# A down product of tokens by channels, added to x1 straight from its PSUM banks

## The reference, cut to what matters

```python
sel = sigmoid(einsum('bsd,ed->bse', x1, expert_sel))
scores = relu(einsum('bsd,edh->bseh', x1, keys))            # the up product, 16 experts of 128
out = einsum('bseh,ehv,bse->bsv', scores, values, sel)      # the down product, summed over experts
x = _layernorm(x1 + out, axis=-1)
```

## Time and profile before

| | |
|---|---|
| median of the runs | 1125.85 us (1124.51 to 1129.42) |
| the profiled execution's span | 1119.6 us |
| PE, matmuls | busy 93%, 5228 of them |
| DVE, ACT, POOL | busy 71%, 47%, 21% |
| mean granted clock of PE | 0.969 of full |
| `down_bank` matmuls | 1536, some 0.40 us each, overlapping |
| copies into `oT` | 597 ns median, two a group |

### The profile page before, as it was taken

How to read it: one execution, slowest core, us unless ns; L and a number is a source line. 1 busy time by engine, 2 the same in 40 slices (tenths; PEclk the granted TensorE clock), 3 DMA queues, 4 the chain that set the end, 5 groups by cost and what they waited for, 6 DMA issues and landing times.

```text
span 1119.6 us, 17488 instructions
## 1 busy us (share of the span) xinstructions
PE 1039.2 (93%) x5228; PEld 871.5 (78%) x5228; DVE 793.8 (71%) x1811; ACT 525.6 (47%) x1223; POOL 234.0 (21%) x280
## 2 busy tenths in 40 slices
PE   5775689999998999989999899999999899999996
PEld 4564568888887888878888788878888788888885
DVE  6844368687875788758787577857887687877564
ACT  5632265346533565235653356334653356534342
POOL 2321222222212111111212121221112221222221
PEclk9987889999999999989999899999999999999999
DMA  5021000020001100011000110011000110000000
GB/s 182 23 95 57 0 2 20 2 76 20 2 21 39 56 1 10 9 40 56 1 19 3 55 38 1 19 39 56 0 1 19 40 56 1 19 1 20 2 20 20
DMA packets 12089, 32.01 MB, mean 29 GB/s; under 512 B 1792, under 2 KB 2048, under 8 KB 12032
## 3 DMA queue, kind: packets, MB, share of 16 engines
q1 hardware_dynamic: 12032, 31.42, 8.3%
HBM read 22.50 MB, written 8.39 MB: 28 GB/s over the span
## 4 chain that ended last, share of the span: by engine, by line
PE 85%; issue 7%; DVE 4%; ACT 2%; POOL 1%; DMA 0%; DVEq 0%; ACTq 0%; SPq 0%; POOLq 0%
PE down_bank L996 30%; PE up_bank L996 30%; PE ring_bank L996 9%; PE qk_bank L996 7%; PE g_bank L996 4%; PE ring_bank L1114 1%; PE ring_bank L1095 1%; DVE gated L970 1%; PE ring_bank L1079 1%; PE ring_bank L1105 1%; PE ring_bank L1104 1%; ACT gated_h L522 1%; PE ring_bank L1060 0%; ACT oT L522 0%; DVE gated_l L980 0%
## 5 line engine op out<-in xcount | busy, mean ns | idle before, releaser
L522 ACT ACTIVATE gated_h<-gated 128x512 fp32r<-128x512 f32 x256 | 161.3, 630 | 443.8 <-DVE gated L970 443.8
L503 POOL PARTITION_BROADCAST sel_all<-sel_rows x240 | 192.2, 803 | 745.1 <-DVE gated L970 718.9
L970 DVE SCALAR_TENSOR_TENSOR gated<-up_bank,sel_all 128x512 f32<-128x512 f32 x256 | 176.1, 688 | 135.8 <-PE up_bank L996 83.2
L996 PE MATMUL down_bank<-gated_h,vals_h 128*128 128x512 f32 x512 | 213.0, 416 | 25.0 <-ACT oT L522 18.7
L980 DVE TENSOR_TENSOR gated_l<-gated,gated_h 128x512 fp32r<-128x512 f32 x256 | 178.9, 699 | 47.0 <-ACT gated_h L522 47.0
L996 PE MATMUL up_bank<-x1T_h,keys_h 128*128 128x512 f32 x512 | 204.4, 399 | 0.0
L996 PE MATMUL down_bank<-gated_h,vals_l 128*128 128x512 f32 x512 | 204.2, 399 | 0.0
L996 PE MATMUL down_bank<-gated_l,vals_h 128*128 128x512 f32 x512 | 204.1, 399 | 0.0
L996 PE MATMUL up_bank<-x1T_h,keys_l 128*128 128x512 f32 x512 | 203.5, 398 | 0.0
L996 PE MATMUL up_bank<-x1T_l,keys_h 128*128 128x512 f32 x512 | 202.3, 395 | 0.0
L996 PEld LDWEIGHTS down_bank<-gated_h,vals_h 128*128 128x128 f32 x512 | 98.2, 192 | 46.2 <-ACT oT L522 19.9
(11 more groups left out here) (159 smaller groups left out, 1720.0 us busy)
## 6 DMA issues: line engine op xcount, KB each, us to landing
xT_raw<-in_xT SPq DMA_DIRECT2D x16, 512.0 KB, 3.8
x_raw<-in_x SPq DMA_DIRECT2D x16, 512.0 KB, 4.5
out<-z SPq DMA_DIRECT2D x32, 256.0 KB, 2.5
oT<-in_keys SPq DMA_DIRECT2D x4, 512.0 KB, 4.0
z<-in_values SPq DMA_DIRECT2D x4, 512.0 KB, 5.4
sel_rows<-sel SPq DMA_DIRECT2D x64, 8.0 KB
x<-in_wqk SPq DMA_DIRECT2D x1, 512.0 KB, 3.4
sel_all<-in_b_qk SPq DMA_DIRECT2D x1, 256.0 KB, 5.2
```

Of the source, the lines that this page charges most:

```text
L503: nc.gpsimd.partition_broadcast(sel_all[:, e % 2], row, P).then_inc(sel_spread, 1)
L522: return nc.scalar.activation(dst, src, ACT.Copy, **kw)
L970: V.scalar_tensor_tensor(out=gated[:], in0=up_bank[s % 2][:], scalar=0.0, in1=sel_all[:, s % 2], op0=ALU.max, op1=ALU.mult).then_inc(gate_ ...
L996: last = mm(dst, lhs, rhs, start=start and i == 0, stop=stop and i == n - 1, **kw)
```

## The change

The down product is turned round. gated is now stationary, 128 tokens at a time (t, 0 to 3), and the 256 channels of vals are streamed, so that the sums stand as tokens by channels: bank a of `down_bank` holds the token blocks 2a and 2a + 1 side by side. A step has 12 matmuls of 256 columns in place of 6 of 512. The first matmul of each bank clears it; the second block's region is then free to be written.

Since the sums stand as the output does, nothing is copied or transposed. DVE adds x1 to each bank straight into `z` (`add_zs`, stage ZA) in the first step behind the group: step 17 for the first group of a batch, step 1 of the next iteration for the second. Its wait is `down_made`, and PE waits for `z_added` before it writes the bank anew. The rest of OT stays where it was, as stage ZN, and takes no ring bank. ACT's copies and PE's transposes go. In the last iteration both adds come first, the first of them as soon as half of the last product is made. `w_room`, of the same size, takes the place of `oT` as landing place.

```diff
 LOOP = dict(
     plan={
-        0: [("QT", 2)], 1: [("QT", 3)], 2: [("OT", 0), ("Y", 4)], 3: [("OT", 1)], 4: [("Y", 5)],
+        0: [("QT", 2)], 1: [("ZA", 0), ("ZA", 1), ("QT", 3)], 2: [("ZN", 0), ("Y", 4)], 3: [("ZN", 1)], 4: [("Y", 5)],
...
-        16: [("GG", 5)], 17: [("QK", 7)], 18: [("GG", 6)], 19: [("KS", 0), ("OT", 0), ("GG", 7)],
-        20: [("OT", 1)], 21: [("KV", 0), ("QT", 0)], 22: [("QT", 1)], 23: [("Y", 0)],
+        16: [("GG", 5)], 17: [("ZA", 0), ("ZA", 1), ("QK", 7)], 18: [("GG", 6)], 19: [("KS", 0), ("ZN", 0), ("GG", 7)],
+        20: [("ZN", 1)], 21: [("KV", 0), ("QT", 0)], 22: [("QT", 1)], 23: [("Y", 0)],
...
-LAST = dict(plan={1: [("OT", 0), ("OT", 1)]}, split_xT={}, split_x={}, bias_x={}, scale_q={},
+LAST = dict(plan={1: [("ZA", 0), ("ZA", 1), ("ZN", 0), ("ZN", 1)]}, split_xT={}, split_x={}, bias_x={}, scale_q={},
...
-RING_KINDS = ("QT", "Y", "XT", "LG", "OT", "KS", "KV")
+RING_KINDS = ("QT", "Y", "XT", "LG", "KS", "KV")
...
         @block.scalar
-                if (s - LAG) % E == E - 1 and step_exists(it, s, LAG):
...
-                        act.wait_ge(down_made, f + 1)
-
-                    at_least(act, o_transposed, 2 * grp)
...
-                    for m in range(M if not last_iteration(it) else 1):
-                        copy(oT[:, m], down_bank[m][:]).then_inc(o_copied, 1)
...
         @block.vector
+            def add_zs(it, s):
+                for kind, a, off in planned(it, s, ("ZA",)):
+                    n = out_pair(it, off, a)
+                    t = GT * (off % G) + 2 * a
+                    if last_iteration(it) and a == 0:
+                        dve.wait_ge(last_half_made, 1)
+                    else:
+                        dve.wait_ge(down_made, it * STEPS + (off + 1) * E)
+
+                    at_least(dve, stored[a], it * (16 * G) + off * 16)
...
+                    V.tensor_tensor(z[:, a].rearrange("p t c -> p (t c)"), down_bank[a][:],
+                                    x1[:, t:t + 2].rearrange("p t c -> p (t c)"),
+                                    ALU.add).then_inc(z_added, 1)
...
+                add_zs(it, s)
                 if step_exists(it, s):
                     f = step_no(it, s)
                     dve.wait_ge(up_made, f + 1)
...
-                if last_iteration(it) and s == LAG - 1:
-                    dve.wait_ge(down_made, B * STEPS)
-                    at_least(dve, o_transposed, 2 * (G * B - 1))
-                    V.tensor_copy(oT[:, 1], down_bank[1][:]).then_inc(o_copied, 1)
...
         @block.tensor
-                    elif kind == "OT":
...
-                                last = nc.tensor.transpose(bk[:, j:j + P], oT[:, m, t * P:(t + 1) * P], ident[:])
-                        last.then_inc(o_transposed, 1)
...
-                    if e == 0:
-
-                        at_least(pe, o_copied, M * grp)
-                    for c in range(M):
-                        r = (s - LAG) % 2
-                        if c == 1 and last_iteration(it):
+                    r = (s - LAG) % 2
+                    for t in range(GT):
+                        a, i = divmod(t, 2)
+                        if e == 0 and i == 0:
+
+                            at_least(pe, z_added, 2 * grp - 1 + a)
+                        if t == 2 and last_iteration(it):
                             last.then_inc(last_half_made, 1)
-                        last = product(down_bank[c][:], [(both(vals_h, vals_l, ALL, e, slice(c * P, (c + 1) * P)),
-                                                          both(gated_h, gated_l, ALL, r, ALL))],
-                                       start=(e == 0), stop=(e == E - 1))
+
+                        last = product(down_bank[a][:, i * C:(i + 1) * C],
+                                       [(both(gated_h, gated_l, ALL, r, slice(t * P, (t + 1) * P)),
+                                         both(vals_h, vals_l, ALL, e, ALL))],
+                                       start=(e == 0 and i == 0), stop=(e == E - 1),
+                                       skip_group_check=True)
                     last.then_inc(down_made, 1)
```

More of the change, by code:

```diff
@@ L121, in stages @@
     for kind, a in schedule(it)["plan"].get(s, ()):
-        if kind == "OT":
+        if kind in ("ZA", "ZN"):
             g = 0 if s >= E else -1
@@ L197, in build_program @@
         gated_h, gated_l = sb("gated_h", [P, 2, GN], F32R), sb("gated_l", [P, 2, GN], F32R)
-        oT = sb("oT", [P, M, GN])
+        w_room = sb("w_room", [P, WPIECE])
         z = sb("z", [P, 2, 2, C])
@@ L259, in build_program @@
         last_half_made = sem("last_half_made")
-        o_copied = sem("o_copied")
-        (o_transposed, z_added, z_stated, z_aggregated, z_rooted, z_inverted, z_shift_made, out_made) = map(sem, (
-            "o_transposed", "z_added", "z_stated", "z_aggregated", "z_rooted", "z_inverted",
+        (z_added, z_stated, z_aggregated, z_rooted, z_inverted, z_shift_made, out_made) = map(sem, (
+            "z_added", "z_stated", "z_aggregated", "z_rooted", "z_inverted",
             "z_shift_made", "out_made"))
@@ L443, in step @@
                     load_half(it, 1)
-                for kind, a, off in planned(it, s, ("LG", "OT")):
+                for kind, a, off in planned(it, s, ("LG", "ZN")):
                     if kind == "LG":
@@ L601, in late @@
             def late(it, s):
-                for kind, a, off in planned(it, s - 1, ("OT",)):
+                for kind, a, off in planned(it, s - 1, ("ZN",)):
                     n = out_pair(it, off, a)
@@ L608, in late @@
                 for kind, a, off in transposed_first(
-                        planned(it, s, ("QK", "GG", "KV", "QT", "Y", "XT", "LG", "OT"))):
+                        planned(it, s, ("QK", "GG", "KV", "QT", "Y", "XT", "LG", "ZN"))):
                     b = it + off
@@ L648, in late @@
                         copy(sel[:], ring_of(it, s, kind, a)[LOW:LOW + E, :]).then_inc(logits_low, 1)
-                    elif kind == "OT":
+                    elif kind == "ZN":
                         n = out_pair(it, off, a)
@@ L807, in early @@
                 for kind, a, off in transposed_first(
-                        planned(it, s - 1, ("QK", "GG", "KS", "KV", "QT", "Y", "XT", "OT"))):
+                        planned(it, s - 1, ("QK", "GG", "KS", "KV", "QT", "Y", "XT", "ZN"))):
                     b = it + off
@@ L867, in early @@
                                        z_rstd[:, a, 1:2]).then_inc(last_out_made, 1)
+            def add_zs(it, s):
[7 more added lines that the diff above has]
+                    at_least(dve, stored[a], it * (16 * G) + off * 16)
+                    if isinstance(it, int) and it == 0:
+                        dve.wait_ge(piece_lo, WPIECES)
+                    V.tensor_tensor(z[:, a].rearrange("p t c -> p (t c)"), down_bank[a][:],
+                                    x1[:, t:t + 2].rearrange("p t c -> p (t c)"),
+                                    ALU.add).then_inc(z_added, 1)
             def late(it, s):
@@ L902, in late @@
                         V.reciprocal(q_scale[:], q_root[:]).then_inc(q_scale_set, 1)
-                for kind, a, off in planned(it, s, ("KS", "KV", "Y", "LG", "OT")):
+                for kind, a, off in planned(it, s, ("KS", "KV", "Y", "LG", "ZN")):
                     b = it + off
@@ L1023, in layer1 @@
             def layer1(it, s):
-                for kind, a, off in planned(it, s, ("QK", "GG", "KS", "KV", "QT", "Y", "XT", "LG", "OT")):
+                for kind, a, off in planned(it, s, ("QK", "GG", "KS", "KV", "QT", "Y", "XT", "LG")):
                     b = it + off
```

11 lines of the change are left out of this document (1 added, 10 removed).

## The result

The changed kernel takes **1107.8 us** (median of 1103.01, 1107.31, 1108.26 and 1110.40), against 1125.24 for the kernel before (four runs): ratio 0.9846, 95% interval 0.9806 to 0.9886, so 1.5% faster. The sign was right; the gain was 17.5 us where 11.1 were expected. Between the two profiled executions it is 18.4 (spans 1119.6 and 1101.2).

What follows compares the result with a forecast made beforehand. Outside five jump waits and the tail, PE's issue was taken as the bound. 2.5 - 13.2 + 1.9 - 2.3 = -11.1 us took the span from 1119.6 to 1108.5, the median to 1114.8; range 1109.5 to 1122.5.

Steps and rivals of the forecast that it cites:

- Term 1: Down product, 12 matmuls of 256 columns for 6 of 512: at KV product's pace +0.01 us a step, +2.5 us.
- Rival A: Down product at the pace of g or Y, 0.02 to 0.04 slower: 1119.7 to 1124.6 us; chance 0.12.
- Term 2: PE's transposes of oT go: 30 stages outside the tail at 0.44 us each, -13.2 us.
- Term 3: Five loop jumps: PE waits for the first z add instead of the oT copy, +0.37 each, +1.9 us.
- Rival B: PE stalls at the jump as DVE does, mostly hidden: up to +5 us, 1119.8; chance 0.10.
- The clock left as it is: Lower clock behind the jumps' stands taken as unchanged, with 3 us of the range given to it.
- Elsewhere, at nothing: ACT's dropped copies, DVE's earlier adds, stores and ring waits outside jumps and tail: no change in time.
- Term 4: Tail: adds take the places of the copies, so the last statistics start earlier, -2.3 us.
- C: DVE sets the pace in steps 19 to 21, so the 0.88 us of transposes isn't gained: +7, 1121.8; chance 0.09.
- D: First load of each down product is exposed, 0.09 us a step: +22.1, 1136.9 us, slower; chance 0.07.
- E: No saving, because the transposes overlapped other PE work: 1125 us; chance 0.02.
- From span to median: Median of the runs taken to lie 6.25 us above the profiled span, turning 1108.5 into 1114.8.

Runs made afterwards that it cites:

- run 9: Changed kernel, loop written out for all four engines, with 32-byte fillers putting every operand on a multiple of 64 bytes: 1084.0 us.
- run 7: Kernel before, loop written out for all four engines, with PE's transposes of oT left out: 1085.0 us.
- run 3: Changed kernel with the loop written out for PE alone; DVE, ACT and SP still jump: 1115.1 us.
- run 12: Kernel before, looped, its down product split into 12 matmuls of 256 columns, nothing turned round, copies and transposes kept: 1122.2 us.
- 5: Kernel before, looped, with SP waiting for DVE's first gate behind the jump before issuing its two 512 KB loads: 1103.9 us.
- run 11: Changed kernel, loop written out for PE alone, with SP issuing its two loads only after the first gate behind the jump: 1094.7 us.
- 6: Changed kernel, looped, with SP waiting for the first gate behind the jump before issuing its two loads: 1104.9 us.
- run 2: Changed kernel with the loop written out for all four engines: 1085.9 us.
- 1: Kernel before with the loop over iterations 1 to 6 written out for PE, DVE, ACT and SP: 1095.8 us.

## Why the prediction was wrong, point by point

- **What bounds the kernel:** right. PE's issue outside the jumps and the tail, 755 of 783 us in six iterations.
- **Term 1, +2.5:** right in kind, small. 0.018 a step in place of 0.01, so about +4.4 for 246 steps. What was wrong in it is the choice of KV as nearest row by its addresses (run 9 refutes that ordering), and that the block behind was left out: the up product pays too. Rival A, 0.03 or 0.05, would have been too much for the turned product, though 0.03 is right for the split one.
- **Term 2, -13.2:** 0.41 a stage by run 7, not 0.44, so -12.3.
- **Term 3, +1.9:** the step that failed, and the one that put the forecast outside its range. It took PE as passing the jump unhindered and DVE's return at 488.3 as given. The stands fell by 6.4 us, an error of 8.3. Rival B had PE's stall, and priced it on the wrong side (0 to +5), because it too kept DVE's return and the add at 491.77 fixed. With these fixed its reckoning holds: PE's 2.3 us lie in the time in which DVE is away, so a microsecond that PE stands early is one less to wait later, and the sum of the stands doesn't fall. What neither had is that DVE comes back sooner when PE fetches: its five returns add up to 26.7 us before and 20.7 after (24.3 in run 3, 21.3 in run 12). These 6.0 us are about the 6.4 by which the stands fell; how they fall jump by jump is not shown, since at three jumps after the lower clock too lies ahead of the down product that needs z and takes from the wait. Run 3, the changed kernel without PE's jump, is close to the machine that the prediction described: 18.6 us on z, forecast 20.6. In the six iterations it takes 775.3 us, where the forecast makes 776.5 (783.2 - 6.7), out of terms that err against each other (issue 1.9 more, stands 2.2 less, clock 1.0 less). That its time, 1115.1 us, is within 0.3 of the forecast is luck: its profiled span is 1113.7, not 1108.5, since its start, up to the loop, is 5.0 longer than before.
- **The clock left as it is:** wrong by 3.9 us in the six iterations. A stand of 2.3 us ahead of the up product, in place of 3.4 to 4.4 ahead of the down product, was followed by 3.4 us at 1.2 GHz at three jumps of five; before it was 3.4, 6.8, 6.8, 3.4 and none. I had given it 3 us of the range; I should have let it hang on the length of the stand. In the looped runs the granted clock fell behind none of the ten stands of 1.2 to 2.0 us (runs 5 and 11), behind 8 of the 16 of 2.2 to 2.8 us (after, 6, 12 and one of 3), and behind 8 of the 9 of 3.4 to 4.4 us (before and 3).
- **Elsewhere, at nothing:** right. In run 2, without jumps, all 32 adds into z make PE wait 0.2 us in all.
- **Term 4, -2.3:** right. 7.8 us from the half product's end to the end of the span, forecast 7.9, before 10.2.
- **Rivals C, D, E:** none happened. The waits for `gated_l` are the same 1.1 us as before.
- **From span to median:** 6.25 us forecast, 6.6 found, by luck. In each run of which both are on record the time is 1.8 us above the span of the same execution; the rest is by how much the profiled execution was quicker than the median (1103.01 against 1107.8), and over the twelve runs the distance goes from -2.3 (run 2) to +4.6 (run 11).

Forecast terms 1, 2 and 4 say -13.0 us, and the straight kernels (1 and 2) differ by 9.9: without jumps I would have expected 3 us too much. With them I expected 6.4 too little (11.1 for 17.5).

The Trainium skill, Runtime: NRT & Kernel Launch, Instruction fetch mechanics, was right that a taken branch costs a fetch and that PE has more room. Its size for PE, 2048 instructions, is not the length up to which a loop runs on here: one of 1744 is fetched anew, with about nine packets of 16 KB an iteration; how large the room is no run measures. And its sentence that crossing from one block of instructions to the next is mostly hidden holds in the straight kernels, where PE has no gap of over 0.15 us in the six iterations.

## What to carry to other kernels

At a hardware loop's jump, look at what the DMA queues carry in those microseconds: a load issued there can hold back the fetch of an engine that has to jump, and moving it behind the first useful instruction may be worth more than work saved. Count each engine's instructions per iteration before adding to them, and price an engine's own stall together with the stalls it lies beside, not on top of them. Where the code fits, write the loop out: the straight changed kernel, 1085.9 us or 3.6% below the kernel before, is faster than every looped one here.

## What the runs showed of the hardware that I had not expected

- PE's loop of 1400 instructions jumps back in 0.3 us, one of 1744 in 3.5 to 3.8, one of 1783 in 3.5 to 4.1, the second with 44 instruction packets of 16 KB in five iterations in place of none.
- DVE's return over a jump takes 2.8 to 3.1 us when no load is issued near it, and 5.0 to 6.1 when two 512 KB loads are issued in the microsecond ahead of its branch, the second in 0.34 us.
- While PE fetches at the jump, SP needs 1.17 to 1.48 us to issue its second load in place of 0.34, in 10 of the 11 jumps of the table at which PE's queue has a packet, and each time DVE's fetch gets through early, 3.7 to 4.6 us. That the slow issue is what lets it through is argued from this coincidence; no run changed it alone.
- Splitting the down product costs 0.018 us a step with the stationary and the streamed operand turned round and 0.032 without (from sums of straight kernels), and a shift of operands by 32 bytes costs 7.7 us in six iterations.
